# Mamba block plus expert FFN on one core: one wait per step for TensorE's four 32-column sums

## What is computed

```python
deltaA  = exp(delta[..., None] * A)                      # 512 channels x 16 states
deltaBx = (delta * xs)[..., None] * B[:, :, None, :]
ys      = scan of  h = deltaA * h + deltaBx  along the 1024 rows
y       = einsum('blcn,bln->blc', ys, C)                 # sum over the 16 states
out     = (y + xs * D) * silu(res);  x + out @ w_out
```

## Time and profile before

| | |
|---|---|
| median of 3 runs | 2160.95 us (2160.07 to 2165.15) |
| the profiled execution | 2160.5 us, span of its instructions 2158.7 us |
| stage 1, steps (first scan to last product) | about 94 to 1143 us of the span |
| mean granted TensorE clock | 0.917 of full speed |
| busy in the span | TensorE matmul 79%, VectorE 61%, ScalarE 41%, GpSimd 40% |

### The profile page before, as it was taken

How to read it: one execution, slowest core, us unless ns; L and a number is a source line. 1 busy time by engine, 2 the same in 40 slices (tenths; PEclk the granted TensorE clock), 3 DMA queues, 4 the chain that set the end, 5 groups by cost and what they waited for, 6 DMA issues and landing times.

```text
span 2158.7 us, 20606 instructions
## 1 busy us (share of the span) xinstructions
PE 1710.6 (79%) x5491; PEld 821.9 (38%) x5492; DVE 1327.1 (61%) x1984; ACT 882.4 (41%) x1598; POOL 862.5 (40%) x399
## 2 busy tenths in 40 slices
PE   7387877878778787787765999949999999999900
PEld 2121312213122131221103767626666666676600
DVE  3379989798797987979994344413333333333345
ACT  4457556574565745657442333301221212212100
POOL 0766849577595775957850222210000000000065
PEclk9699989999899898998997999979999999999955
DMA  4633425334253342533416510010110101101033
GB/s 125 144 77 92 106 55 141 80 93 103 56 141 80 93 103 56 140 79 93 102 39 220 192 39 29 30 66 25 34 33 31 34 31 33 32 31 34 25 114 122
DMA packets 105433, 169.86 MB, mean 79 GB/s; under 512 B 14624, under 2 KB 53264, under 8 KB 105248
## 3 DMA queue, kind: packets, MB, share of 16 engines
q1 hardware_dynamic: 99232, 152.44, 27.3%
q0 software_dynamic: 6144, 16.79, 2.4%
HBM read 127.76 MB, written 41.42 MB: 78 GB/s over the span
## 4 chain that ended last, share of the span: by engine, by line
PE 52%; DVE 26%; ACT 8%; issue 7%; POOL 3%; DMA 3%; SPq 1%; another core or an unknown queue 0%; DVEq 0%; ACTq 0%; POOLq 0%
DVE psH L900 17%; PE psA L1382 12%; PE psP L1399 12%; DVE X L909 6%; PE psP L1228 5%; PE psP L1307 5%; PE psH L1316 5%; PE psA L1265 5%; PE psH L1390 3%; ACT psH L746 2%; PE psP L1217 2%; POOL gat L460 1%; PE psP L1236 1%; ACT L746 1%; DMA ud_dram<-ud 1%
## 5 line engine op out<-in xcount | busy, mean ns | idle before, releaser
L407 POOL TENSOR_TENSOR X<-rep,B 128x2048 f32<-128x2048 f32 x128 | 577.0, 4522 | 246.0 <-PE psA L1265 231.9
L1265 PE MATMUL psA<-X,gsum 128*32 128x512 f32 x1024 | 466.0, 677 | 238.7 <-DVE X L909 238.6
L746 ACT ACTIVATE psH<-rep,A_q 128x512 f32<-128x512 f32 x512 | 349.9, 689 | 123.6 <-DVE X L909 114.6
L900 DVE TENSOR_TENSOR_SCAN psH<-psH,X 128x512 f32<-128x512 f32 x256 | 313.0, 1223 | 119.6 <-ACT psH L746 75.6
L900 DVE TENSOR_TENSOR_SCAN psH<-psH,carry,X 128x512 f32<-128x512 f32 x256 | 329.8, 1288 | 48.0 <-ACT psH L746 48.0
L909 DVE TENSOR_TENSOR X<-psH,C 128x512 f32<-128x512 f32 x512 | 347.3, 679 | 0.0
L460 POOL DMA_INDIRECT gat<-eo_dram,slots x64 | 62.7, 980 | 664.9 <-DVE slots L1143 644.4
L1265 PEld LDWEIGHTS psA<-X,gsum 128*32 128x32 f32 x1024 | 59.7, 113 | 618.7 <-DVE X L909 575.9
L1382 PE MATMUL psA<-ew_s,nTb 128*128 x576 | 268.1, 608 | 0.8 <-ACT nTb L821 0.8
L1399 PE MATMUL psP<-ew_s,hT 128*128 x1152 | 262.2, 381 | 2.6 <-ACT hT L827 2.6
L1399 PEld LDWEIGHTS psP<-ew_s,hT 128*128 128x128 f32 x1152 | 220.0, 191 | 63.3 <-issue 36.8
(11 more groups left out here) (172 smaller groups left out, 1597.3 us busy)
## 6 DMA issues: line engine op xcount, KB each, us to landing
rep<-ud_dram SPq DMA_DIRECT2D x128, 512.0 KB, 8.7
ud_dram<-ud SPq DMA_DIRECT2D x32, 512.0 KB, 5.0
ew_s<-in_L_ffn_ew_dram SPq DMA_DIRECT2D x16, 1024.0 KB
xb<-rows_dram SPq DMA_DIRECT2D x72, 128.0 KB, 2.0
eo_dram<-eo SPq DMA_DIRECT2D x72, 128.0 KB, 1.7
B<-bc_dram SPq DMA_DIRECT2D x128, 64.0 KB, 2.3
C<-bc_dram SPq DMA_DIRECT2D x128, 64.0 KB, 2.1
out_dram<-fin SPq DMA_DIRECT2D x8, 512.0 KB
```

What stands on the lines that cost most here:

```text
L407: nc.gpsimd.tensor_tensor(X[:, Q % NX], rep[:, g % 2, 1], B4[:, f:f + 1, :].broadcast_to([P, NR, TC]), ALU.mult).then_inc(bx_ready, 1)
L746: nc.scalar.activation(psH[:, r, :], rep[:, g % 2, 0, r, :], ACT.Exp, scale=A_q[:, c, r, f:f + 1]).then_inc(dA_ready, 1)
L900: nc.vector.tensor_tensor_scan(psH[:, r, :], psH[:, r, :], X[:, Q % NX, r, :], start, ALU.mult, ALU.add).then_inc(scan_done, 1)
L1265: ins = nc.tensor.matmul(psA[r * GJ:(r + 1) * GJ, g % 2, :], gsum[:], X[:, Q % NX, r, :], start=False, stop=(f == NF - 1), skip_group_chec ...
```

## The change

```diff
             def add_state(k, q):
                 c, f = q // NF, q % NF
                 g, Q = k * CH + c, k * NQ + q
+                pe.wait_ge(hc_ready, Q * NR + NR)
                 for r in range(NR):
-                    pe.wait_ge(hc_ready, Q * NR + r + 1)
                     ins = nc.tensor.matmul(psA[r * GJ:(r + 1) * GJ, g % 2, :], gsum[:], X[:, Q % NX, r, :],
                                            start=False, stop=(f == NF - 1), skip_group_check=True)
                 ins.then_inc(y_acc, 1)
```

## The result

The changed kernel took 2194.7 us, median of 4 runs (2191.37 to 2196.09); the kernel before took 2162.43 us beside it (2160.07 to 2165.15). The ratio is 1.0143, 95% interval 1.013 to 1.0157. It is slower by 32 us. The forecast was slower by 26 us, 2187 us, within 2170 to 2220 us. The profiled execution of the changed kernel is its fastest run, 2191.37 us, with a span of 2189.6 us, against 2158.7 us before.

What follows compares the result with a forecast made beforehand. VectorE was taken to set the pace in stage 1, TensorE mattering only where ScalarE reads it. Terms 4.5 + 9.1 + 9.1 + 1.6 + 2.0 = 26.3 us on 2160.5 us gave 2187 us, range 2170 to 2220 us.

Steps and rivals of the forecast that it cites:

- The sum itself: Sums after the last product: eight instructions in 1.06 us against a pair's 1.04 us, price 0.02 us at either clock.
- The gaps: Step 11 to next tile's step 1, and steps 7 to 9: TensorE idles, so sums start at 1.2 GHz.
- Step 1: T0 behind the sums of step 0 runs at the low clock in all seven preparing tiles: 4.5 us together.
- Step 8: X0 runs partly at half speed after the sums: 1.3 us in each of seven tiles, 9.1 us.
- Step 9: D1 and the sums of step 8 ahead of it slow down: 1.3 us in each of seven tiles, 9.1 us.
- Steps 2 and 3: I1 and the sums behind it run low in one more tile: 1.6 us, bounds 0 and 8 us.
- The end: Last sums at the low clock, 0.8 us, and last output projection losing 1.2 us: 2.0 us.
- Steps 4 to 6: Within steps 3 to 6, TensorE idles about 1.7 us before the last product, too short to matter: 0.
- the much slower case: Rival: the loop of steps 3 to 6 also loses its clock, 48 us more, 2235 us; chance 0.10.
- The faster case: Rival: four sums side by side keep the clock up better than spread pairs, 10 us gained, 2150 us; chance 0.04.
- The case of no change: Rival: the clock holds, or all that it slows is covered, 2160 to 2167 us; chance 0.09.

Runs made afterwards that it cites:

- the faster version: Kernel before, its own waits, plus multiplications by zeros in steps 12, 15, 0, 7, 9 and two between I0 and I1: 2152.36 us, repeated 2151.15 us.
- the joint waits with fillers: Changed kernel plus zero pairs at the old waits outside steps 1 to 6 and the fillers of the faster version: 2165.47 us, ratio 1.002.

## Why the prediction was right

**The sum itself: right.** Eight sums took 1.06 us at the high clock, as foretold, and 1.93 us at the low one, 0.1 us more: the row of 1.84 us was an eight in whose course the clock rose again, and the trace of before has one that was low throughout. No step with nothing but sums changed its length, no wait of VectorE between 300 and 1065 us names GpSimd, and the joint wait in steps 3 to 6 was free.

```profile
513.22 1.94 PE L1265 MATMUL psA<-X,gsum 128*32 128x512 f32 x8
```

**The gaps: right, and shown.** The clock fell in the quiet steps and, of the dense steps 3 to 6, in one place only (tile 0, at step 6). Joint steps cost only where T0, X0 or D1 stands behind them, and work put back into the gaps brought X0 and D1 back to 3.71 and 1.12 us. One reading behind it was loose: of the 587 to 690 us of the earlier trace rows more than half are dense steps of the next tile. The part that bears it out is steps 11 to 0, 586.9 to 630.2 us, where the clock was 1.00. The warning of the Trainium skill, "TensorE: Matmul & The Clock Gate", section "Why this matters for your kernels", against idle gaps between bursts, agrees with this trace, and stands here with its price: 32 us of 2162.

**Step 1: mis-sized, 4.5 us foretold, 6.1 us measured.** The place was right, but I took the tiles that already ran low as the full price. They were low for a part only: step 1 is now 9.81 to 9.83 us in all seven tiles, 1.35 us above the high ones (8.46 and 8.48 us), and the tiles that had been low paid 0.1 to 0.4 us too.

**Step 8: near, 9.1 foretold, 10.8 measured.** X0 was at 3.63 us in six tiles before and at 3.75 us in tile 3; now it takes 4.52 to 5.46 us, 0.9 to 1.8 us more by tile and 9.1 us more in sum, just the term that was foretold. The other 1.7 us were left out: the sums ahead of X0, too, had been at the high clock, wholly or in part, in some tiles, and now take 1.93 us in all. That the middle of the bounds met the X0 term so exactly is luck; only its bounds had been worked out.

**Step 9: mis-sized, 9.1 foretold, 12.9 measured.** The step of the working that failed is "this one falls about when the sums start. [...] I take 1.3 us". It falls before them, in every tile: step 9 grew by 1.83 or 1.84 us in each of the seven, which is the upper bound of 1.75 us and a little more. The run with step 8 alone shows the same 12.9 us.

**Steps 2 and 3: wrong sign, 1.6 us foretold, -1.2 us measured.** The low stretch at I1 in tiles 3 and 5 went away. The output projection now ends later, after its low start (8.11 us, to 523.3 us), and leaves a shorter gap between I0 and I1 (1.46 us, 2.17 us in the earlier trace rows). The run with steps 12 to 0 joint bears this out: in tile 3 the output projection took 8.12 us, the gap was 1.44 us and I1 came high, while in tiles 1 and 5 it took 7.14 us, the gap was 2.17 us and I1 ran low. What step 2 lost, 2.4 us, had been left out.

**The end: right, with luck**, 2.3 against 2.0 us; the same place cost 3.9 us and 3.3 us in two of the other runs.

**Steps 4 to 6: foretold free, 2.2 us measured.** 1.7 us of it is one low stretch in step 6 of tile 0. The same step of the same tile is 1.7 us longer in both other runs that keep the joint wait in steps 1 to 6 and have no filler there, and in no run besides, the one with steps 3 to 6 joint included. So this small piece of the much slower case looks like a real cost of the change; which of the waits makes it was not tried.

Taken together, every place but steps 2 and 3 was foretold too low, and the sum of 26.3 us came out 4.6 us short of the trace and 6 us short of the medians.

The faster case was ruled out as soon as the clock fell in the quiet steps. The case of no change was ruled out by the waits of VectorE: the longer wait of the low tiles in the earlier trace rows now stands in step 1 of every tile (2.60 or 2.86 us).

## What to carry to other kernels

An engine that is not the bound can still have a duty in its gaps: small pieces of TensorE work spread over a step hold its clock for the one projection that everything waits for. Before work is bunched, ask what runs first after the gap that this leaves, and who waits for it. And where a critical matmul follows a known gap, a few multiplications by zeros ahead of it can be worth more than they cost, provided that they end before the real work is ready.

## What the runs showed beside it

- Four 32-column sums on four column groups ran side by side (eight instructions in 1.06 us), but zero pairs on one and the same 32 columns one behind the other, 0.43 us an instruction at the high clock. Where several pairs are ready at once this turned free filler into 35 us of hold-up.
- In the run with only step 8 joint, 3.80 us without work were enough, in all seven tiles, for the next sums and D1 to run at 1.2 GHz, although TensorE had worked for most of the 10 us before. Also half the joining, sums every 3.6 us, did not hold the clock.
- Where low stretches fall is partly chance. Two executions of the faster version, the one profiled in each of its runs, differ by 2.8 us in steps 2 and 3 of tile 0: in the second the sums and I0 ran low there (sums 1.92 us, I0 3.78 us). Step 3 was low in two, three, five or no tiles in the kernels here, 1.6 us each. So a total alone can't tell causes of a few microseconds apart. Whether this is why the joint waits with fillers spread over 13 us from run to run (2159.47 to 2172.7 us) and the faster version over 4 and 7 us was not tried.
